# Expert lists in 16 blocks of 512 rows and 7 of 256, marks made by units, and the logits' pieces placed anew in a macaron transformer kernel

## What is computed

```
x = x + 0.5 * moe(layernorm(x))      # shared MLP + the two best of 8 experts per token
x = x + mixing(layernorm(x))         # 8 heads: h = a*h + b along 1024 tokens, then projections and an MLP
x = x + 0.5 * moe(layernorm(x))      # the same weights again
x = x + 0.5 * ffn(layernorm(x))      # MLP with weights of -1, 0, 1
x = x + linear_attention(layernorm(x))
x = x + 0.5 * ffn(layernorm(x))
```

## Time and profile before

| | |
|---|---|
| median of 3 runs | 1185.23 us (1183.57 to 1189.68) |
| the profiled execution, its own time | 1186.23 us |
| its span, first to last instruction | 1184.5 us |
| PE busy | 1066.8 us (90%) |
| DVE busy | 840.4 us (71%) |
| POOL busy | 683.2 us (58%) |
| ACT busy | 669.8 us (57%) |
| mean granted TensorE clock | 0.954 |

### The profile page before, as it was taken

How to read it: one execution, slowest core, us unless ns; L and a number is a source line. 1 busy time by engine, 2 the same in 40 slices (tenths; PEclk the granted TensorE clock), 3 DMA queues, 4 the chain that set the end, 5 groups by cost and what they waited for, 6 DMA issues and landing times.

```text
span 1184.5 us, 16414 instructions
## 1 busy us (share of the span) xinstructions
PE 1066.8 (90%) x4800; PEld 731.3 (62%) x4800; DVE 840.4 (71%) x2362; ACT 669.8 (57%) x1265; POOL 683.2 (58%) x786
## 2 busy tenths in 40 slices
PE   6779999998989999999979979999967678999996
PEld 6336778875657677667745448888734445555553
DVE  6785787767867887787765967777762676767661
ACT  2336767765566676667543338777744445545533
POOL 4006556637998888877662046666465665754330
PEclk9989999999999999999987989999996888989998
DMA  8666667741000000000001036877510000000000
GB/s 270 240 261 210 213 214 246 239 127 29 14 14 13 14 14 12 15 5 1 1 19 54 1 117 213 252 241 241 162 53 19 16 16 25 25 12 10 10 18 18
DMA packets 67976, 108.81 MB, mean 92 GB/s; under 512 B 8336, under 2 KB 46224, under 8 KB 67856
## 3 DMA queue, kind: packets, MB, share of 16 engines
q1 hardware_dynamic: 57904, 87.30, 22.1%
q0 software_dynamic: 9984, 20.47, 6.8%
HBM read 81.00 MB, written 28.57 MB: 93 GB/s over the span
## 4 chain that ended last, share of the span: by engine, by line
PE 58%; POOL 17%; DVE 11%; issue 6%; ACT 5%; DMA 2%; POOLq 0%; SPq 0%; DVEq 0%; ACTq 0%
PE bank L193 7%; PE bank L426 3%; PE bank L427 3%; PE bank L428 3%; PE bank L443 3%; PE bank L445 3%; PE bank L444 3%; POOL wr L642 3%; PE bank L1071 3%; PE bank L1077 3%; PE bank L1596 3%; PE bank L424 2%; PE bank L1111 2%; PE bank L1617 2%; POOL got L642 2%
## 5 line engine op out<-in xcount | busy, mean ns | idle before, releaser
L586 POOL DMA_INDIRECT spare_all<-xs,list_row x184 | 191.7, 1042 | 210.9 <-DVE list_row L724 107.4
L781 DVE TENSOR_TENSOR hid_lo<-hid,hid_hi 128x512 fp32r<-128x512 f32 x184 | 127.0, 692 | 75.0 <-ACT hid L528 73.4
L528 ACT ACTIVATE hid<-bank,b_up_of 128x512 f32<-128x512 f32 x184 | 125.6, 684 | 6.5 <-PE bank L428 1.2
L527 ACT ACTIVATE hid_hi<-bank,b_up_of 128x512 fp32r<-128x512 f32 x138 | 95.3, 690 | 47.7 <-PE bank L428 35.2
L642 POOL DMA_INDIRECT got<-ys,y_slots x80 | 87.3, 1091 | 51.0 <-issue 40.7
L193 PEld LDWEIGHTS bank<-ident,spare_all 128*128 128x128 f32 x504 | 64.8, 150 | 78.0 <-issue 57.6
L193 PE MATMUL bank<-ident,spare_all 128*128 128x128 f32 x504 | 82.1, 289 | 26.1 <-DVE spare_all L372 18.0
L1190 ACT ACTIVATE gate_b<-bank,head_rstd 128x128 f32<-128x128 f32 x256 | 73.0, 370 | 55.7 <-POOL head_rstd L1297 55.2
L528 ACT ACTIVATE hid<-bank,cols_sb 128x512 f32<-128x512 f32 x64 | 43.9, 687 | 88.4 <-PE bank L424 79.4
L426 PE MATMUL bank<-xh,wr 128*128 128x512 f32 x184 | 82.4, 448 | 3.5 <-DVE xl L774 3.5
L1863 DVE TENSOR_TENSOR gate_b<-bank,spare_all 128x512 f32<-128x512 f32 x64 | 43.1, 687 | 50.2 <-PE bank L1617 48.0
(11 more groups left out here) (291 smaller groups left out, 2749.0 us busy)
## 6 DMA issues: line engine op xcount, KB each, us to landing
wr<-wq SPq DMA_DIRECT2D x92, 512.0 KB, 4.7
ys<-spare_all SPq DMA_DIRECT2D x46, 256.0 KB, 5.3
wq<-wr SPq DMA_DIRECT2D x16, 512.0 KB, 5.7
got<-in_w_mlp SPq DMA_DIRECT2D x8, 512.0 KB, 5.9
xs<-spare_all SPq DMA_DIRECT2D x16, 256.0 KB, 2.3
spare_all<-xs,list_row POOLq DMA_INDIRECT x184, 3.7
out_x<-X SPq DMA_DIRECT2D x8, 256.0 KB, 2.3
ys<-in_x SPq DMA_DIRECT2D x1, 1792.0 KB, 10.5
```

The source lines that it names most:

```text
L528: nc.scalar.activation(hid[:, n % HC], bank[up_bank(n)][:], ACT.Gelu_apprx_tanh, bias=bias).then_inc(s["gelu_done"], 1)
L586: g.indirect_dma_start(out=xin[:, j % XIN, b], out_offset=None, in_=xs, in_offset=bass.IndirectOffsetOnAxis(ap=list_row[:, n:n + 1], axis=0))\
L781: v.tensor_tensor(hid_lo[:, q], hid[:, n % HC], hid_hi[:, q].bitcast(F32), ALU.subtract).then_inc(s["lo_done"], 1)
```

## The change

The lists are 16 blocks of 512 rows (`FULL`) and 7 of 256 (`HALVES`), 23 as before. An expert gets pairs of 256-row units as 512-row blocks, and an odd unit as a 256-row block; `SLOTS` gives the order of work: three full ones and a half, four times, then four full ones, then three halves. The instructions of a half list have 256 columns or 2 blocks instead of 512 or 4; each half list still loads its expert's whole weights. `COLUMNS` falls from 92 to 78. `find_spots`, `find_experts` and `find_stores` get further small instructions on DVE. `mark` makes the marks of columns for a unit with one instruction (the token number goes over to the marks of rows). In the tail of the mixing part, the roots of tiles 0 to 5 are one pair of instructions on POOL, statistics and normalizations are put in groups, tiles 0 to 3 alone are turned there, and tiles 4 to 7 are turned ahead of the second MoE part's step 0. In the last pipeline the beats 0 to 8 get an order of their own on PE and ACT, `sums(0)` moves from beat 9 to beat 8, and the gathers of tile 2 all lie in beat 5, behind that beat's roots. The rows of tile 1 are added in beat 5, not 4.

The diff, cut to its core:

```diff
-    LISTED = TOP * TOKENS // TW + EXPERTS - 1
+    FULL, HALVES = TOP * TOKENS // TW, EXPERTS - 1
+    LISTED = FULL + HALVES
+    LIST_ROWS = FULL * TW + HALVES * TW // 2
+    SLOTS = [s for q in range(4) for s in (3 * q, 3 * q + 1, 3 * q + 2, FULL + q)] + list(range(12, FULL)) + list(range(FULL + 4, LISTED))
...
+    def width(j):
+        return TW if SLOTS[j] < FULL else TW // 2
...
-        marks_hi = sb("marks_hi", [P, 2, TB, COLUMNS], F16)
...
+        marks_hi = sb("marks_hi", [P, 2, COLUMNS, TB], F16)
...
-                    ins = nc.tensor.matmul(bank[6][:, TW - COLUMNS:], marks_lo[:, u % 2, m], marks_hi[:, u % 2, m],
+                    ins = nc.tensor.matmul(bank[6][:, TW - COLUMNS:], marks_lo[:, u % 2, m], marks_hi[:, u % 2, :, m],
...
-                turn(pe, bank[7], lambda b: xin[:, j % XIN, b]).then_inc(s["taken"], 1)
+                turn(pe, bank[7], lambda b: xin[:, j % XIN, b], width(j) // P).then_inc(s["taken"], 1)
...
-                nc.tensor.matmul(out[:], w_up(j, 0, c), xh[:, j % 2], start=True, stop=False)
...
+                nc.tensor.matmul(out[:, 0:width(j)], w_up(j, 0, c), xh[:, j % 2, 0:width(j)], start=True, stop=False)
...
-                for n in range(2):
-                    step(n)
-                turn_for_route(pe, s, TILES - 1)
+                for i in range(TURNED_AHEAD, TILES):
+                    turn_for_route(pe, s, i)
+                    if i > TURNED_AHEAD:
+                        find_logits(pe, s, i - 1)
                 find_logits(pe, s, TILES - 1)
-                for n in range(2, HC):
+                for n in range(HC):
                     step(n)
                 find_places()
...
+            for i in range(0 if first else TURNED_AHEAD, TILES):
...
-                steps.link(v.tensor_tensor(over[:], upto[:, :, BLOCKS - 1:BLOCKS].broadcast_to([P, EXPERTS, TILES]), block_starts[:], ALU.is_gt))
-                steps.link(v.tensor_reduce(blocks_of[:], over[:], AX_X, ALU.add))
...
+                steps.link(v.tensor_scalar(units[:], upto[:, :, BLOCKS - 1], TW / 4 - 0.5, 2.0 / TW, ALU.add, ALU.mult))
...
+                steps.link(v.tensor_scalar(pairs[:], units[:], 0.5, -0.25, ALU.mult, ALU.add))
...
+                steps.done(v.scalar_tensor_tensor(singles[:], pairs[:], -2.0, units[:], ALU.mult, ALU.add))
+                steps.link(v.tensor_tensor_scan(ends[:], every[:, 0:EXPERTS], pairs[:], 0.0, ALU.mult, ALU.add))
...
+                steps.done(v.tensor_tensor_scan(single_ends[:], every[:, 0:EXPERTS], singles[:], 0.0, ALU.mult, ALU.add))
...
+                steps.link(v.tensor_tensor(single_off[:], single_ends[:], singles[:], ALU.subtract))
+                steps.link(v.tensor_scalar(units[:], single_off[:], HALVES - 0.5, -float(HALVES + 2), ALU.is_gt, ALU.mult))
...
+                steps.done(v.tensor_copy(upto_tile[:].rearrange("p i e -> p e i"), upto.rearrange("p e (i b) -> p e i b", b=TB)[:, :, 0:SOON, TB - 1]))
...
+                by_expert = lambda a: a.unsqueeze(1).broadcast_to([P, BLOCKS, EXPERTS])
+                steps.link(v.tensor_tensor(ranked, place[:], by_expert(pairs_end[:]), ALU.is_ge))
+                steps.link(v.tensor_tensor(ranked, ranked, by_expert(single_off[:]), ALU.mult))
+                steps.link(v.tensor_tensor(place[:], place[:], ranked, ALU.add))
...
+                steps.done(v.tensor_copy(spot_hi16[:], spot_hi[:]))
...
-                for m in range(TB):
-                    at = u * TB + m
-                    v.tensor_scalar(marks_lo[:, u % 2, m], column_no16[:], spot_lo[:, at:at + 1], None, ALU.is_equal)
-                    ins = v.tensor_scalar(marks_hi[:, u % 2, m], column_no16[:, 0:COLUMNS], spot_hi[:, at:at + 1],
-                                          token_no[:, at % BLOCKS:at % BLOCKS + 1], ALU.is_equal, ALU.mult)
+                at = u * TB
+                by_block = spot_hi16[:, at:at + TB].unsqueeze(1).broadcast_to([P, COLUMNS, TB])
+                v.tensor_tensor(marks_hi[:, u % 2], column_by_block[:], by_block, ALU.is_equal)
+                for n in range(at, at + TB):
+                    ins = v.tensor_scalar(marks_lo[:, u % 2, n - at], column_no16[:], spot_lo[:, n:n + 1],
+                                          token_no[:, n % BLOCKS:n % BLOCKS + 1], ALU.is_equal, ALU.mult)
...
+                steps.link(v.tensor_scalar(single_ends[:], single_ends[:], past_full[:, 1:2], None, ALU.add))
+                steps.link(v.tensor_tensor(past[:, 0:HALVES], half_no[:], single_ends[:].unsqueeze(1).broadcast_to(of_half), ALU.is_ge))
...
+                steps.link(v.tensor_scalar(tab_f[:, HALVES:2 * HALVES], half_no[:, :, 0], past_full[:, 1:2], None, ALU.is_ge))
+                steps.link(v.tensor_tensor(tab_f[:, 0:HALVES], tab_f[:, 0:HALVES], tab_f[:, HALVES:2 * HALVES], ALU.mult))
+                steps.link(v.tensor_tensor(expert_of[:, FULL:], expert_of[:, FULL:], tab_f[:, 0:HALVES], ALU.add))
+                steps.link(v.tensor_scalar(expert_of[:], expert_of[:], float(EXPERTS - 1), None, ALU.min))
...
-                steps.link(v.tensor_scalar(tab_f[:], expert_of[:], float(EXPERTS - 1), None, ALU.min))
...
+                steps.wait()
+                v.tensor_copy(tab[:], expert_of[:]).then_inc(s["table_ready"], 1)
...
+                steps.done(v.tensor_tensor(beyond[:], upto_tile[:], paired[:].unsqueeze(1).broadcast_to([P, SOON, EXPERTS]), ALU.is_gt))
...
+                steps.done(v.tensor_reduce(beyond_any[:], beyond[:], AX_X, ALU.max))
...
+                steps.link(v.scalar_tensor_tensor(blocks_upto[:], beyond_any[:], FULL + 1.5, blocks_upto[:], ALU.mult, ALU.max))
...
-                    steps.link(v.tensor_copy(hid_hi[:, q], hid[:, n % HC]))
...
+                    steps.link(v.tensor_copy(hid_hi[:, q, 0:w], hid[:, n % HC, 0:w]))
...
-            return n - begin if 0 <= n - begin < TILES - 1 else None
...
+        NORMS_AHEAD = {HEADS + 3: (0, 1, 2), HEADS + 5: (3, 4, 5), HEADS + 7: (6,)}
+        TURNS_AHEAD = {HEADS + 5: (0, 1), HEADS + 8: (2, 3)}
+        LOGITS_AHEAD = {HEADS + 6: (0,), HEADS + 7: (1,), HEADS + 11: (2,), HEADS + 12: (3,)}
...
-                if tile_ahead(n, LOGITS_AHEAD) is not None:
...
+                    pe.wait_ge(s["ab_out"], 2 * HEADS)
+                for i in LOGITS_AHEAD.get(n, ()):
+                    find_logits(pe, after, i)
+                for i in TURNS_AHEAD.get(n, ()):
...
-                if tile_ahead(n, STATS_AHEAD) is not None:
-                    find_rstd(pool, steps, after, tile_ahead(n, STATS_AHEAD))
+                if n == HEADS + 2:
+                    find_rstd(pool, steps, after, 0, ROOTS_AHEAD)
...
+            return beat < CHUNK_0
+        def parts_at(beat):
+            if beat < CHUNK_0 - 4:
+                return []
+            if beat == CHUNK_0 - 4:
+                return range(TOP * TB, 2 * TOP * TB)
+            first = {CHUNK_0 - 3: 0, CHUNK_0 - 2: 0, CHUNK_0 - 1: 2, CHUNK_0: 4, CHUNK_0 + 1: 4}
+            at = 2 * TOP * TB + sum(n for b, n in first.items() if b < beat) + 2 * max(0, beat - CHUNK_0 - 2)
+            return [n for n in range(at, at + first.get(beat, 2)) if n < TOP * TB * (TILES - 1)]
         kv = [w[:].rearrange("p (h a) e -> p h (a e)", h=2) for w in (wa, wb)]
...
                 turned = chunk_at(beat - 1)
-                if g is not None:
+                if fills(beat):
+                    if here(TURN_LA) is not None:
+                        l1_take(pe, s, here(TURN_LA), 1, bank[4])
+                    if here(VK) is not None:
+                        project(here(VK), V)
+                        project(here(VK), K)
+                    if here(BACK_1) is not None:
+                        ff_back(here(BACK_1), 0)
+                    if here(QS) is not None:
+                        project(here(QS), Q)
+                        sums(0)
+                        project(here(QS), QT)
+                    if here(UP_1) is not None:
+                        ff_up(here(UP_1), 0)
+                    if here(DOWN_1) is not None:
+                        ff_down(here(DOWN_1), 0)
+                    if here(TURN_1) not in (None, 0):
+                        ff_turn(here(TURN_1), 0)
+                    continue
+                if g is not None and g > 0:
...
-                ahead, part_no = divmod(2 * beat + TOP * TB // 2, TOP * TB)
-                if beat > STATS_1 and ahead + 1 < TILES:
-                    for n in (part_no, part_no + 1):
-                        moe_fetch(pool, moe, ahead + 1, n, FETCHED_WIDE)
+                if not fills(beat):
+                    for n in parts_at(beat):
+                        moe_fetch(pool, moe, 1 + n // (TOP * TB), n % (TOP * TB), FETCHED_WIDE)
                 if here(BACK_1) is not None:
                     root(here(BACK_1), 1)
                 if here(STATS_1) is not None:
                     root(here(STATS_1), 0)
...
+                    for n in parts_at(beat):
```

(4 more changed lines are left out.)

193 lines of the change are left out of this document (122 added, 71 removed).

## The result

| | kernel before | changed kernel |
|---|---|---|
| median of the first measurement | 1187.45 us (1183.57 to 1191.49, 4 runs) | 1161.47 us (1157.30 to 1163.46, 4 runs) |
| ratio, 95% interval | | 0.9764 (0.9738 to 0.9791) |
| the profiled execution, its own time | 1186.23 us | 1161.6 us |
| its span | 1184.5 us | 1159.9 us |
| PE busy, mean clock | 1066.8 us, 0.954 | 1031.4 us, 0.950 |

The kernel is faster, as forecast. The forecast was 1143 us (1129 to 1161) and the first measurement 1161.5, half a microsecond above the range. The kernel before stood higher in that measurement too (1187.45 us, not the 1185.23 the forecast started from): as a ratio the range is 0.953 to 0.980, and 0.9764 lies inside it, near its upper end. In two later sessions the same kernel took 1143.5 and 1146.3 us. So one question of this study is where 17 us of one and the same program come and go.

The account below looks back on a forecast made before the run. PE, busy 90% of the span, bounds the lists; chains through DVE, POOL and ACT pace mixing's tail and the last pipeline's start. Terms -42 + 1 + 3 + 2 + 1.5 - 4 - 3.5 = -42 gave 1143 us (1129 to 1161).

Parts of the forecast that it names:

- The sum: Whole kernel: all terms together -42 us, from the profiled execution's 1186.2 to 1144.2, given as 1143 us.
- rival (a): Lists: half list bound elsewhere, by ACT or the gather, 4.9 us each, total 1163 us; chance 0.14.
- The lists: Both MoE parts: a half list takes 3.45 us on PE instead of 6.46, 14 halves saving 3.0 each, -42 us.
- (c): Lists: fp32r products at 256 columns lose their rate, half list 10.7 us, total 1245 us; chance 0.03.
- (d): Both MoE parts: added DVE chain costs 5 us more than its bounds in each, total 1153 us; chance 0.10.
- (b): More paid back: second pointer free (-3), power short (-4), pipeline gains its bound (-4.5), total 1131 us; chance 0.11.
- Full after half: Lists: copy and difference of full width must fit short steps where a half precedes a full list, +1 us.
- Setup pieces: First MoE part's lists: PE reaches `back` some 2 us sooner after pieces 0 and 4 and waits longer, +3 us.
- Places and marks: Ahead of the lists: marks begin 4.0 us later, each unit 0.25 less; +2 us first part, +1.5 second.
- Tail of mixing: End of mixing: fewer turns and logits between the last tile's steps, 24-column root taken as 4 us; -4 us.
- Last pipeline: Start of last pipeline: root and turn come earlier, chunk 0 ends about 6 us sooner, 2 to 5 remain; -3.5 us.
- its sentence that PE's rows in the lists stand 0.12 to 0.13 apart: Sign of being right: this spacing in half lists, no wait over 0.5 us outside the setup pieces.

Follow-up runs that it names:

- second profile: Changed kernel measured again unaltered in a further session, against the kernel before: 1143.52 us, ratio 0.9639; this is its profile.
- the half lists last: Changed kernel with the 16 full lists first and the 7 half lists at the end: 1147.57 us (0.9638), then 1137.16 us (0.9588).
- the marks alone: Kernel before with only the marks made by units, on 92 columns: 1183.19 us, ratio 0.9952.
- The timed part alone: Kernel before with only the mixing tail changed (roots of six tiles together, tiles 4 to 7 turned ahead of step 0): 1184.66 us, ratio 0.9968.
- The timed pairs: New order of pipeline beats 0 to 8 only, against kernel before: 0.9999; old beats in the kernel with half lists at the end: 1141.06 against 1137.16 us.
- the first session: Four kernels on one chip, against the kernel before: half lists at the end 0.9638, tail only 0.9968, pipeline order only 0.9999, marks by units only 0.9952.
- an experiment that "cured" the waits here: Changed kernel with a full list behind a half one turned, copied and its low part made one step earlier: 1147.90 us, ratio 0.9697.

## Why the prediction was right, and what it did not foresee

**The sum (-42): right, and partly by luck.** By the stages of the second profile the change is 1.6 ahead of the lists, -39.2 in the lists and behind them, +1.2 in mixing, +0.7 in marks and -5.8 in the last pipeline: -41.5 us. The forecast has 2 - 38 - 4 + 1.5 - 3.5. So 5 us that mixing didn't give in that profile were made up by the other four terms. The first measurement's 1161.5 us stands close to rival (a)'s 1163, but for another reason: half lists take 3.51 us there too.

**The lists (-42, right).** In the second profile the two lists' stretches are 19.2 and 19.8 us shorter, with the stages behind them 0.4 shorter and 0.2 longer: -39.2 where the forecast has -42 + 1 + 3 = -38. A half list takes 3.51 us, not 3.45. Where the forecast has 127.5 us for all lists, part 2 takes 129.7 and 128.3. Three rivals fall: (a) half lists are not bound elsewhere, and seven in a row still average 3.6 behind the first, (c) the pitch is 0.12, (d) the chain cost what was said. Of (b) the cheap second pointer is refuted below.

**Full after half (+1).** About 0.6 in part 1, nothing in part 2, and the lists' stages are no longer with 7 such places than with 4.

**Setup pieces (+3, measured 2.2).** PE waits on them 1.52 + 2.54 + 0.56 = 4.6 us in the second profile, against 0.44 + 1.48 + 0.54 before. As forecast, the `back` behind pieces 0 and 4 waits longer (second profile):

```profile
151.00 1.12 PE L208 MATMUL bank<-ident,part 128*128 128x128 f32 x4 [2.54 <-DVE part L868]
```

**A missed term: the stores.** I followed gather, copy and difference into the lists, but not the gathers out of them. `rows_stored` lets tile 0 be gathered once the block is stored that holds the last expert's first rows. That is about block 14, in the new order the list at place 18, and behind it lie one full and three half lists instead of five full ones. With the half lists last the two stages take 17.2 us instead of 18.9 to 20.8 and 19.2: 4 to 6 us that were to be had. The sum doesn't feel it: the forecast left these two stages as they were, and against the kernel before they are 0.4 shorter and 0.2 longer in the second profile.

**Places and marks (+2 and +1.5, measured +1.2 to +1.6 and -0.3 to +0.7).** DVE in part 2, first profile; PE's second product of `find_places` starts at 641.22:

```profile
642.72 0.42 DVE L723 TENSOR_TENSOR wz<-wz 128x256 f32<-128x256 f32 x1
643.06 0.16 DVE L725 TENSOR_SCALAR units<-wz 128x8 f32<-128x8 f32 x1
643.26 0.17 DVE L726 TENSOR_SCALAR units<-units 128x8 f32<-128x8 f32 x1
...
651.57 0.32 DVE L772 TENSOR_TENSOR marks_hi<-column_by_block,spot_hi 128x312 f16<-128x312 f16 x1
651.80 0.98 DVE L774 TENSOR_SCALAR marks_lo<-column_no,spot_lo,token_no 128x128 f16<-128x128 f16 x4
652.69 0.32 DVE L772 TENSOR_TENSOR marks_hi<-column_by_block,spot_hi 128x312 f16<-128x312 f16 x1
```

The marks begin 10.4 us behind it instead of 6.6 (654.52 to 661.08): 3.8 later, forecast 4.0. A unit takes 1.12 us, not 1.2 to 1.3. The prediction's sum for part 1 doesn't come out of its own terms: 12 units at 0.25 less, one in three of them hidden, return 2 to 3 us, not 3.5. What came back is 4.7, as the marks alone show, so the chain behind them cost more than the 1.5 that it was given; +2 came out by errors that partly cancel. The instruction with two pointers takes the 0.22 from start to start that the earlier trace rows gave for it. What I overpriced is the one over 312 columns: 0.23 us, where I had 0.24 to 0.40. The Trainium skill, "VectorE: DVE Perf Modes", in its perf-mode tier table, gives a `tensor_tensor` of 16 bits the doubled rate, and the rows agree: from start to start L772 takes 0.23 us for 312 elements, L723 in fp32 0.34 for 256; the fourfold rate that it gives to `tensor_scalar` is not reached by L774, 128 columns in 0.22 us, so that a unit at 0.9 stays refuted.

**Tail of mixing (-4, right when timed alone).** The root of 24 columns takes 4.20 us (first profile); I took 4:

```profile
602.56 4.20 POOL L396 TENSOR_TENSOR rstd_all<-ve_all,neg_half 128x24 f32<-128x24 f32 x1
```

The first turn waits for it, and the statistics queue behind it as said:

```profile
608.05 2.10 PE L208 MATMUL bank<-ident,spare_all 128*128 128x128 f32 x8 [2.95 <-DVE spare_all L401]
612.03 1.11 PE L208 MATMUL bank<-ident,t_sb 128*128 128x128 f32 x4 [1.88 <-DVE t_sb L1504]
```

The timed part alone gives 3.8 us (1.3 to 6.2). In the traces it hides behind the clock, below.

**Last pipeline (-3.5, not settled).** In all ten traces with the new order `read_out(0)` comes 38.4 to 40.1 us behind the pipeline's first turn, in the four with the old one 42.6 to 44.0. That is 2.5 us sooner at least; the prediction had about 6 for the end of chunk 0. In eight of the ten the stage takes 305.6 to 307.3 us, with the old order 310.9 to 318.8. First profile:

```profile
871.59 1.12 PE L208 MATMUL bank<-ident,t_sb 128*128 128x128 f32 x4 [6.10 <-ACT t_sb L1809]
875.03 1.09 PE L208 MATMUL bank<-ident,xn 128*128 128x128 f32 x4 [2.33 <-ACT xn L1809]
```

The timed pairs say 0.0 (up to 2.9) and 1.4 to 3.9. What the start gains can be lost to the clock later: the two other traces, both with the half lists last, take 310.9 and 314.6 us, and their last 111 to 114 us ran at a mean clock of 0.92 and 0.90, against 0.97 in the last 106 us of the second profile of the changed kernel. Whether the order brings such stretches about is not shown.

**What the prediction did not foresee in the first measurement** goes against its sentence that PE's rows in the lists stand 0.12 to 0.13 apart with no wait above 0.5 us outside the setup pieces. In that profile the lists' stages are 5.2 and 11.5 us longer than in the second one, the stages behind them 2.3 and 3.6; mixing and marks are 5.1 and the rest 0.5 shorter: 17.0 in all. The prediction took the signal from PE to ACT as a constant. It is one in the profile before, and in eight of the thirteen profiles of this study. Late copies (over 0.6 us behind the last transpose) were in the first profile of the changed kernel (18 of 46) and in all four of the first session (4, 1, 1 and 2), and in none of the eight of the three later sessions. Each session ran on another chip, so session and chip can't be told apart.

The kernel may have a part in it as well. In the first session the kernel before took 1188.0 us (28 runs), in the later ones 1186.6 to 1187.4: about 1 us more. The halves-last kernel took 10 us more there (1147.6 against 1137.2), of which its two profiles show 2.2 and 8.0 in the lists' stages, and the changed kernel 17 us more in its first measurement. Whether it is the half lists that attract late signals, or the chip of the first measurement that had more of them, can't be told from one profile each.

What holds the signals is open. One rival was not tested, the recording of the profile itself. The traces list the semaphore updates that were recorded: 8345 to 8500 in the five profiles with late copies, 11965 to 11983 in the eight others and 12375 in the profile before. So where signals came late, some three in ten of these records are missing too, and this holds for all kernels of the first session alike.

**Faster than both kernels:** the half lists last, 0.9588 and 0.9638 in its two sessions, against 0.9639 and 0.9644 of the changed kernel without late signals; in pairs of shortest runs, 1135.5 against 1140.1 us. The two orders never ran in one session without late signals, and the intervals of 0.9588 and 0.9639 touch (0.9619 and 0.9595), so this is likely, not shown. The stages of the lists' ends give 4 to 6 us for it, the stores' wait.

## What to carry to other kernels

Before explaining a wait by the program, run the same program again in another session: an experiment that "cured" the waits here (a ratio of 0.9697, inside the expected range) had cured nothing, since the same waits were gone from the unchanged program too. Look at what the trace has lost as well: the profiles with late signals were those with missing records. Compare stages, not totals: the stage that an edit can't touch is the control that every trace brings along. And when blocks get shorter, follow not only what feeds them but also what waits for them to be finished: with less work behind a store, a wait that had 9 us of room has none.

## What the runs showed of the hardware

**A signal of PE can be late.** From PE's last transpose to ACT's copy it is 0.31 us as a rule. In five profiles it was now and then more, up to 5.8 us. In the case shown above hardly anybody was busy (windows of 2 us, first profile; PE, PEld, DVE, ACT, POOL, clock, DMA share):

```profile
696.00:698.00 2.00, 1.77 (x9) 0.96 (x7) 0.00 (x0) 0.00 (x0) 0.76 (x1) 1.00 0.23 66
698.00:700.00 2.00, 0.00 (x0) 0.00 (x0) 0.64 (x1) 1.25 (x3) 0.00 (x0) 0.95 0.00 0
```

DVE and ACT have nothing to do from 696 to 698, and DMA stands at a share of 0.23 and then 0.00 (0.97 and 0.77 from 690 to 694). In the case of 5.8 us, in the profile of the marks alone, the DMA share was 0.83 to 0.26 meanwhile. So a load of that moment does not explain both. The signals were held as a queue: the trace has the updates of five PE instructions, which began at 694.80, 695.38, 696.04, 696.80 and 697.37, at 698.72, 698.77, 698.82, 698.88 and 698.93. Signals of ACT were not late: where DVE waited for a copy to make xl, it began 0.03 us behind the copy's end in every profile. The Trainium skill, "Perfetto Trace Analysis" (per-engine timelines), says that a TensorE row's start is the start of its reading and its end is estimated, and that the signal leaves only when PSUM has acknowledged the writes. By that a late signal leaves no mark on PE's own rows, and the trace agrees: PE's rows run on at their usual pace until PE itself has to wait.

**The clock takes or gives some 5 us in the tail of mixing.** Windows of 30 us of the tail, first and second profile of the changed kernel (PEclk is the last column but two):

```profile
596.00:626.00 30.00, 21.36 (x75) 13.11 (x73) 18.33 (x86) 8.98 (x21) 11.31 (x12) 0.72 0.21 61
626.00:656.00 30.00, 27.52 (x115) 15.72 (x114) 21.80 (x84) 11.63 (x17) 1.26 (x2) 0.94 0.03 10
```

```profile
590.00:620.00 30.00, 21.33 (x77) 13.42 (x76) 17.20 (x77) 8.13 (x17) 11.01 (x12) 0.72 0.22 61
620.00:650.00 30.00, 28.91 (x102) 18.64 (x101) 18.93 (x70) 11.07 (x16) 1.26 (x2) 0.77 0.03 10
```

About the same instructions run at a mean clock of 0.94 in the one and of 0.77 in the other: a further stretch at 1.2 GHz falls on them. In kernels with the new tail, the stage from mixing's first turn to `find_places` takes 376.4 to 378.6 us in the five profiles whose clock was full from 60 to 40 us ahead of `find_places`, and 381.9 to 384.3 in the six where it was 0.91 to 0.93 there. The kernel before has 381.4 with the full clock there, so like against like the new tail is 3 to 5 us shorter. A change of 4 us in such a place can't be read from two traces that differ in their clock; it took 12 timed runs.
